# Filling block-diagonal keys by four GpSimd copies in place of four transfers, with the key turn one step later on VectorE

## The reference

```
def modulated(x, s, aff_w, aff_b, w):      # three times, with own weights
    style = s @ aff_w.T + aff_b
    demod = rsqrt(sum((w * style) ** 2) + 1e-8)
    return einsum(x * style, w) * demod

x = x + clip(modulated(x, ...) + bias, -256, 256)          # L0
kx = modulated(x, ...) + k_b                               # K: q = k = v = kx
kx = kx.reshape(B, N, 16 heads, 32)
scores = einsum("bnhd,bnjd->bnhj", kx, kx) / sqrt(32)      # 16 x 16 for each token
out = einsum("bnhj,bnjd->bnhd", softmax(scores), kx)
x = x + modulated(out, ...) + o_b                          # O
```

## Time and profile before

| | us |
|---|---|
| median of 3 runs | 739.38 |
| the runs | 739.37 to 746.77 |
| the profiled execution | 738.66 |
| its span, first to last instruction | 736.9 |
| TensorE busy | 693.7 |
| VectorE busy | 538.0 |
| ScalarE busy | 517.2 |
| GpSimd busy | 4.3 |

### The profile page before, as it was taken

The page is one execution under the profiler, slowest core; times in us unless marked ns, Lnnn a source line. Parts: engine busy times, 40 slices in busy tenths (PEclk is TensorE's granted clock), DMA queues, the critical chain, the costliest instruction groups (busy, mean ns, idle before and its releaser), DMA issues.

```text
span 736.9 us, 21634 instructions
## 1 busy us (share of the span) xinstructions
PE 693.7 (94%) x8886; PEld 673.5 (91%) x8886; DVE 538.0 (73%) x1048; ACT 517.2 (70%) x1040; POOL 4.3 (1%) x11
## 2 busy tenths in 40 slices
PE   7998988999999999999999999999998999989796
PEld 6998888899999999999899989989998999989685
DVE  3668766777778887677788767778876778877662
ACT  4786665767877776677777767778765777766673
POOL 2000000000000000000000000000000000000000
PEclk8999998999999999999999999999999999999999
DMA  9267897798879887888888779689778888876874
GB/s 291 82 172 183 223 238 167 198 240 231 234 220 249 227 205 200 229 230 227 234 227 233 207 201 237 203 242 234 199 199 225 235 229 230 231 194 154 221 217 131
DMA packets 235811, 157.16 MB, mean 213 GB/s; under 512 B 143297, under 2 KB 225217, under 8 KB 235713
## 3 DMA queue, kind: packets, MB, share of 16 engines
q1 hardware_dynamic: 235712, 155.78, 78.3%
HBM read 71.85 MB, written 67.11 MB: 189 GB/s over the span
## 4 chain that ended last, share of the span: by engine, by line
DMA 26%; PE 26%; SPq 17%; DVE 13%; ACT 12%; issue 5%; ACTq 0%; DVEq 0%
PE lin_ps L420 19%; DMA k_turned<-kx 9%; DMA k_bd<-k_rhs 8%; DMA yr<-y_turned 5%; PE s_ps L465 4%; SPq L247 4%; SPq L269 4%; SPq L237 4%; SPq L261 3%; DMA y_turned<-y 2%; ACT y_hi L516 2%; ACT kx L507 2%; ACT x_hi L516 2%; PE y_ps L483 2%; DVE x L761 2%
## 5 line engine op out<-in xcount | busy, mean ns | idle before, releaser
L420 PE MATMUL lin_ps<-x_hi,w_hi 128*128 128x256 f32 x1008 | 287.2, 285 | 5.7 <-DVE w_lo L712 3.5
L420 PE MATMUL lin_ps<-x_lo,w_hi 128*128 128x256 f32 x1008 | 283.0, 281 | 0.0
L420 PE MATMUL lin_ps<-x_hi,w_lo 128*128 128x256 f32 x1008 | 282.7, 281 | 0.0
L420 PEld LDWEIGHTS lin_ps<-x_hi,w_hi 128*128 128x128 f32 x1008 | 191.1, 190 | 13.1 <-issue 12.9
L420 PEld LDWEIGHTS lin_ps<-x_lo,w_hi 128*128 128x128 f32 x1008 | 191.2, 190 | 0.0
L420 PEld LDWEIGHTS lin_ps<-x_hi,w_lo 128*128 128x128 f32 x1008 | 191.2, 190 | 0.0
L420 PE MATMUL lin_ps<-y_hi,w_hi 128*128 128x256 f32 x528 | 150.2, 284 | 7.1 <-DVE y_lo L683 7.1
L420 PE MATMUL lin_ps<-y_lo,w_hi 128*128 128x256 f32 x528 | 149.1, 282 | 0.0
L420 PE MATMUL lin_ps<-y_hi,w_lo 128*128 128x256 f32 x528 | 149.0, 282 | 0.0
L516 ACT ACTIVATE x_hi<-x,style 128x256 fp32r<-128x256 f32 x252 | 113.1, 501 | 46.3 <-DVE x L761 39.5
L683 DVE SCALAR_TENSOR_TENSOR x_lo<-x,style,x_hi 128x256 fp32r<-128x256 f32 x252 | 107.1, 477 | 7.5 <-ACT x_hi L516 7.5
(11 more groups left out here) (59 smaller groups left out, 668.5 us busy)
## 6 DMA issues: line engine op xcount, KB each, us to landing
x<-xT SPq DMA_DIRECT2D x32, 512.0 KB, 7.3
k_turned<-kx SPq DMA_DIRECT2D x32, 512.0 KB, 4.4
k_st<-k_turned SPq DMA_DIRECT2D x128, 128.0 KB, 3.2
k_bd<-k_rhs SPq DMA_DIRECT2D x128, 128.0 KB, 5.0
v_turned<-k_rhs SPq DMA_DIRECT2D x32, 512.0 KB, 6.1
k_v<-v_turned SPq DMA_DIRECT2D x128, 128.0 KB, 3.3
y_turned<-y SPq DMA_DIRECT2D x128, 128.0 KB, 3.0
yr<-y_turned SPq DMA_DIRECT2D x32, 512.0 KB, 5.4
```

The costliest lines, as they stand in the source:

```text
L420: mm = pe.matmul(lin_ps[:, n % NLB, 0:T], w[:, k, m * P:(m + 1) * P], r[:, k, :], start=(q == 0), stop=(q == len(passes) - 1))
```

## The change

In each chunk the four transfers of `spread_k` on SyncE are gone. GpSimd does four `tensor_copy` instead, one for each group of 32 partitions by 1024 elements, behind a wait for `turn_k` of the chunk. `scores` waits for the four copies. GpSimd has no other work after its memsets. In `dve_steps` `turn_k` moves behind the second half of `x1_lo_of`; the lists of the head and the tail stay.

```diff
-            def spread_k(c):
-
-                if c == 0:
-                    sp.wait_ge(g_zero, 1)
-                sp.wait_ge(v_krhs, c + 1)
-                for r in range(R):
-                    sp.dma_start(k_bd[HD * r:HD * (r + 1), r], k_rhs[HD * r:HD * (r + 1)]).then_inc(ld_kbd, DMA)
-
...
             for i in range(FIRST_LOOP, last - 1):
...
                 load_x(i + 2)
-                spread_k(i - 1)
                 v_to_dram(i - 1)
                 store(i - 4, 0, 1)
...
             pool.memset(k_bd[:, :, :, :], 0.0).then_inc(g_zero, 1)
+
+            def spread_k(c):
+
+                pool.wait_ge(v_krhs, c + 1)
+                for r in range(R):
+                    pool.tensor_copy(k_bd[HD * r:HD * (r + 1), r], k_rhs[HD * r:HD * (r + 1)]).then_inc(g_kbd, 1)
+
+            pool.wait_ge(g_zero, 1)
+            for c in range(N):
+                spread_k(c)
...
-                pe.wait_ge(ld_kbd, DMA * R * (c + 1))
+                pe.wait_ge(g_kbd, R * (c + 1))
...
-                    (c0, x1_lo_of, 0), (c1, turn_k), (c0, x1_lo_of, 1), (c2, spread_probabilities), (c4, finish, 0),
+                    (c0, x1_lo_of, 0), (c0, x1_lo_of, 1), (c1, turn_k), (c2, spread_probabilities), (c4, finish, 0),
```

More of the change, by code:

```diff
@@ L137, in build @@
         ld_x = [sem(f"ld_x{i}") for i in range(2)]
-        ld_kbd = sem("ld_kbd")
         v_out_landed, v_in_landed = sem("v_out_landed"), sem("v_in_landed")
@@ L143, in build @@
         g_eps, g_pad, g_warm, g_zero = sem("g_eps"), sem("g_pad"), sem("g_warm"), sem("g_zero")
+        g_kbd = sem("g_kbd")
         v_odd = sem("v_odd")
@@ L306, in _ @@
             load_x(4)
-            spread_k(0)
             v_to_dram(0)
@@ L312, in _ @@
             load_x(5)
-            spread_k(1)
             v_to_dram(1)
@@ L319, in _ @@
             y_to_dram(0)
-            spread_k(2)
             y_from_dram(0)
@@ L327, in _ @@
             y_to_dram(1)
-            spread_k(3)
             y_from_dram(1)
@@ L336, in _ @@
             y_from_dram(2)
-            spread_k(4)
             v_to_dram(4)
@@ L354, in _ @@
             y_from_dram(last - 4)
-            spread_k(last - 2)
             v_to_dram(last - 2)
@@ L360, in _ @@
             y_to_dram(last - 3)
-            spread_k(last - 1)
             y_from_dram(last - 3)
@@ L367, in _ @@
             store(last - 5, 0, 1)
-            spread_k(last)
             y_to_dram(last - 2)
```

## The result

| | before | after |
|---|---|---|
| median, us | 743.08 (4 runs) | 762.3 (4 runs, 760.73 to 764.73) |
| ratio to before, 95% interval | | 1.033 (1.028 to 1.038) |
| profiled execution, us (span) | 738.66 (736.9) | 764.73 (762.9) |

The change makes the kernel 3.3% slower by the ratio on record; the two medians shown give 2.6%, the two profiled executions 3.5%. The forecast was 724. The median of before shown here has one run more than the one ahead of the prediction.

A forecast was written before the change was run, and what follows sets the result against it. TensorE was taken as the bound, stalled in the loop by late `k_bd` transfers: 738.66 - 15.4 (loop stalls) - 1.5 (tail) + 1.5 (allowance) = 723.3, set at 724 us because the runs' median was 0.7 higher; range 718 to 765.

The forecast's parts named there:

- What bounds the kernel: TensorE, busy 94% of the span; in the loop it waited only at `scores` for the `k_bd` transfers, 13.1 us.
- the 15.4 us of the loop's stalls: TensorE's 13 loop waits for `k_bd`, 13.1 us, plus 0.18 us for each, 2.3 us; all forecast to go.
- The key turn 1.0 us later: On VectorE, the turn behind the second half of x1_lo was to end at 335.2 in place of 334.19.
- The copies take 4 us: On GpSimd, four `k_bd` copies a round were to take 4 us, done 3 us before they are due.
- the 7.1: Time in us for the copies, from the moved key turn's end at 335.2 to `scores` due at 342.29.
- I take a loss below 1.9 us, which costs nothing: VectorE's loss per round beside GpSimd's copies was assumed to stay within the cover ahead of `v`.
- Rival A: VectorE is held up by the copies ahead of `v` and `pv` stalls 1.6 us a round: 762 us; chance 0.22.
- the cover of 1.9: Slack in us between `v` being ready and `pv` using it: 2.1, or 1.9 after the shift of 0.2.
- B: VectorE loses 2.2 to 2.8 us; `pv`'s new stall about pays for the old: 730 to 747 us; chance 0.15.
- C: GpSimd's copies starve behind VectorE, making `scores` 2.7 us late a round: 788 us; chance 0.07.
- D: Copies take 7 us or more, or another `scores` input comes last; the stall stays: 735 to 745 us; chance 0.04.
- The tail: At the last `scores`, a gain of 1.5 us was taken; 1.5 us was allowed for the one before and VectorE's losses.

## Why the prediction was wrong, step by step

- **What bounds the kernel, and the 15.4 us of the loop's stalls: right.** With the stall taken away and none put in its place (the copies behind `p_bd`), a round took 20.80 us, where 20.8 was forecast, and the kernel 724.6 (ratio 0.975), where 724 was forecast (0.979).
- **The key turn 1.0 us later: right** in size (6.97 us from its end to `scores`, 8.10 before), and by itself it holds nobody up (ratio 0.992). I had not seen that with transfers they then land 1.1 us sooner, nor that with copies it puts the fourth copy over `finish`, which makes 1.016 into 1.033.
- **The copies take 4 us: nearly.** The page of the changed kernel has them as

```profile
L383 POOL COPY k_bd<-k_rhs 32x1024 f32<-32x1024 f32 x128 | 147.4, 1151 | 568.1 <-DVE k_rhs L733 562.5
```

  and the first four, with VectorE elsewhere, took 4.40 us from start to end. Inside the loop it is 4.78, ready 2.3 us before `scores` was due by the 7.1. Busy time and 128 times the mean agree (147.4 and 147.3), so copies on different partitions do not overlap, and what the page "GPSIMD Engine Reference" of the Trainium skill (section Instruction dispatch) would allow, as I read it, did not happen here.
- **"I take a loss below 1.9 us, which costs nothing": the step that failed.** The loss is 3.2 us, by 2.34 in `p_bd` and 0.88 in `finish`. I had both ends, nothing and the whole of the copies, and took the low one because no row showed the two engines together. Absence of such a row was no evidence, since GpSimd did nothing in the loop. The rule of the Trainium skill (page "SBUF — State Buffer", section SBUF: two separate sides) that I named as speaking against the change was the better guide, and the trace agrees that `p_bd` and `finish` take turns with the copies; only the turns are not quite exclusive, since a pair of copy and `p_bd` takes 1.18 us and not the 1.43 of both alone.
- **Rival A, at 762 us: what happened.** Its loss was put at 3.5 and its cover at 1.9, so 1.6 over; measured 3.2 and 1.6, so 1.6 over. The two errors cancel, so it is luck that its 762 is met to the microsecond. The head's 4.7 us less and the tail's 5.0 us more, for neither of which it had a term, cancel by luck too. The cover is smaller because `pv` starts 0.26 us behind the end of `v` (348.80 to 349.06), which the cover of 1.9 did not allow for.
- **Rivals B, C and D: not seen.** B's loss of 2.2 to 2.8 us is that of three copies (740 us, no change), as B had it. Against C, GpSimd wasn't starved: a copy took 1.03 us alone and at most 1.46 beside VectorE. Against D, the wait for `k_bd` is gone from the loop.
- **The tail: wrong in sign.** The last `scores` waits 3.7 us, where before it was 3.15 and I had taken 1.5 off, because four copies there took 4.7 us. Even with copies of 4 us my own reading gave a gain of 0.3, and nothing supported the 1.5. The head I had put at nothing without a reason.

The chances were 0.22 for A and 0.30 for slower (A and C add up to 0.29), and the range's top of 765 held the result, so the mechanism was on the page with too little weight.

## What to carry to other kernels

Work given to an idle engine isn't free if it lengthens the instructions of a busy one: ask which of the neighbour's instructions lie over it, how much they lose, and what stands behind them. Here the same copies cost 3.3% at one place and gained 2.5% at another 1.65 us later. Before choosing between two routes for four equal pieces, try to split them, since two pieces on each route fitted under the cover of both.

## What the runs showed of the hardware

- GpSimd's copy of 32 x 1024 float32 takes 1.03 us, and four follow each other at 1.1 us. Four memsets of that size, undisturbed, took 3.95 us (0.95 each).
- One such instruction costs VectorE about 0.77 us if it meets a tensor_scalar of 128 x 512 that alone takes 0.48 and follows its neighbour at 0.40, and 0.83 to 0.88 us if a copy meets a tensor_tensor of that size; GpSimd it costs 0.1 to 0.4 us. In a row a pair of copy and tensor_scalar takes 1.18 us, less than the 1.43 of both alone, so the two are not strictly one after the other.
- What is met depends on the form: tensor_scalar meets copies and memsets, tensor_tensor and scalar_tensor_tensor with two inputs in SBUF meet copies only, the transposes (STREAM_TRANSPOSE of 128 x 512 into `v`) meet neither.
- The transfers into `k_bd` landed 1.1 us sooner (5.5 to 4.4, one trace each) when issued 1 us later behind a load of 512 KB. That the load is the cause isn't shown.
